# Second normalised rows moved from VectorE to ScalarE, and the projection of step 6 split straight from PSUM

## The reference

```
x = x + attention(layernorm(x), ctx)           # 16 heads of 64, 128 keys each
h = layernorm(x)                               # (x - mean) / sqrt(var + 1e-5)
logits = h @ Wg.T + bg                         # 16 experts, the best two are taken
x = x + sum over the two of weight_e * (gated(h @ Wgu[e] + bgu[e]) @ Wd[e] + bd[e])
```

## Time and profile before

| | us |
|---|---|
| median of 3 runs | 682.69 |
| lowest and highest | 680.43, 684.36 |
| the profiled execution | 684.96 |
| its span (first to last instruction) | 683.2 |

### The profile page before, as it was taken

One profiled execution on the slowest core, in us unless ns is written; L12 is line 12 of the kernel. 1 busy time (PEld: TensorE's weight loads), 2 busy tenths in 40 slices (PEclk: granted clock), 3 DMA queues, 4 the chain that ended last, 5 costly groups with the idle time before them and its releaser, 6 DMA issues.

```text
span 683.2 us, 20288 instructions
## 1 busy us (share of the span) xinstructions
PE 580.7 (85%) x6823; PEld 468.9 (69%) x6824; DVE 553.7 (81%) x1534; ACT 509.3 (75%) x1411; POOL 450.6 (66%) x551
## 2 busy tenths in 40 slices
PE   0787899999999999999999999998873898989900
PEld 0456688888888888888888888886762476666600
DVE  5776799899898998989989999887995387778605
ACT  0665698999999999999999999986971276767600
POOL 2353557678788787887878878874536157777740
PEclk9977899999999999999999999999996899999955
DMA  8700385007003300600700420181000243333139
GB/s 237 199 1 1 109 319 200 1 10 258 20 11 141 128 10 32 245 9 11 259 19 10 180 89 11 68 266 22 17 8 26 60 108 96 94 87 90 47 93 279
DMA packets 58962, 66.12 MB, mean 97 GB/s; under 512 B 6084, under 2 KB 38620, under 8 KB 58868
## 3 DMA queue, kind: packets, MB, share of 16 engines
q1 hardware_dynamic: 45268, 52.13, 23.7%
q0 software_dynamic: 4608, 8.47, 3.7%
q10 hardware_dynamic: 8992, 4.30, 2.3%
HBM read 19.09 MB, written 46.83 MB: 96 GB/s over the span
## 4 chain that ended last, share of the span: by engine, by line
PE 66%; DVE 14%; issue 8%; DMA 4%; ACT 2%; POOL 2%; SPq 1%; ACTq 1%; POOLq 0%; DVEq 0%
PE bank L1068 15%; PE bank L1069 14%; PE bank L1070 14%; PE bank L1157 9%; PE bank L1207 4%; PE bank L1232 3%; PE bank L1240 2%; DMA ctx_sb<-results 2%; DVE o_nat L949 2%; DMA ctx_sb<-in_ctx_dram 2%; PE bank L1289 2%; PE bank L1267 1%; DVE y L944 1%; DVE oT L883 1%; ACT v L424 1%
## 5 line engine op out<-in xcount | busy, mean ns | idle before, releaser
L476 ACT ACTIVATE probs<-bank,nbias 128x128 f32<-128x128 f32 x512 | 146.0, 368 | 4.1
L592 POOL TENSOR_TENSOR qk<-qkf,zeros 128x512 f16<-128x512 f32 x90 | 115.9, 1287 | 46.8 <-ACT qkf L419 45.4
L679 POOL DMA_INDIRECT results<-z,stage x80 | 80.9, 1011 | 43.4 <-ACT z L513 24.8
L595 POOL TENSOR_TENSOR qk<-qkf,qk 128x512 f16<-128x512 f32 x90 | 104.2, 1158 | 7.1
L908 DVE TENSOR_TENSOR pT<-bank,pT 128x512 f16<-128x512 f32 x128 | 87.7, 685 | 16.0 <-ACT pT L488 13.5
L1068 PE MATMUL bank<-qk 64*128 64x128 f16 x512 | 95.5, 222 | 0.0
L1070 PE MATMUL bank<-qk 64*128 64x128 f16 x512 | 94.4, 219 | 0.0
L1069 PE MATMUL bank<-qk 64*128 64x128 f16 x512 | 94.3, 219 | 0.0
L1157 PE MATMUL bank<-ident,probs 128*128 128x128 f32 x512 | 87.2, 295 | 1.9 <-DVE pT L908 1.9
L887 DVE TENSOR_REDUCE qmax<-bank 128x4 f32<-128x512 f32 x128 | 87.3, 682 | 1.2 <-PE bank L1070 1.1
L488 ACT ACTIVATE pT<-bank 128x512 f16<-128x512 f32 x128 | 76.9, 601 | 11.0 <-PE bank L1157 7.1
(11 more groups left out here) (202 smaller groups left out, 1890.4 us busy)
## 6 DMA issues: line engine op xcount, KB each, us to landing
places<-z SPq DMA_DIRECT2D x8, 4160.0 KB
stage<-places SPq DMA_DIRECT2D x80, 65.0 KB, 1.9
ctx_sb<-results SPq DMA_DIRECT2D x16, 256.0 KB, 5.4
ctx_sb<-in_ctx_dram ACTq DMA_DIRECT2D x4, 512.0 KB, 10.6
stage<-in_L_ffn_Wgu_dram SPq DMA_DIRECT2D x1, 2048.0 KB, 8.7
out_dram<-x_sb ACTq DMA_DIRECT2D x8, 256.0 KB, 5.3
stage<-in_L_xattn_W_qkv_dram SPq DMA_DIRECT2D x3, 512.0 KB, 6.6
results<-z,stage POOLq DMA_INDIRECT x80, 2.3
```

Of the source, the lines that this page charges most:

```text
L476: last = nc.scalar.activation(probs[:, b, k, :], score_bank[b][:, k * P:(k + 1) * P], ACT.Exp, bias=nbias[:, b, k:k + 1], scale=exp_scale)
L592: nc.gpsimd.tensor_tensor(qk_item(par, t, HI), each, zeros[:, :].rearrange("p (i n) -> p i n", i=2), ALU.add).then_inc(s["qk_high"], 1)
L595: nc.gpsimd.tensor_tensor(qk_item(par, t, LO), each, qk_item(par, t, HI), ALU.subtract).then_inc(s["qk_split"], 1)
L679: nc.gpsimd.indirect_dma_start(out=results, out_offset=bass.IndirectOffsetOnAxis(ap=to, axis=0), in_=z[:, (u - 5) % NZ, t, :], in_offset=None,
```

## The change

Piece 6 of each pair's queries and keys joins `DIRECT`. And the two row tiles of y are made by ACT, at the end of its step 7, as scale * x + bias with scale `rstd2` and bias `shift2` = -mean * rstd, for which POOL gets a new function `row_shift2` behind `inverse_root` in step 6. DVE no longer makes y; its casts L980 wait for ACT's `y_ok`.

```diff
-        DIRECT = (1, 4)
+        DIRECT = (1, 4, 6)
...
+                    if r == 7 and pair_live(p - 1):
+                        wait(act, "shift2_ok", p)
+                        wait(act, "yT_mm", p - 1)
+                        wait(act, "yhalf", p * 2 - 2)
+                        wait(act, "ylow", p * 2 - 2)
+                        for j in range(2):
+                            nc.scalar.activation(y[:, j, :], x_sb[:, p * 2 - 2 + j, :], ACT.Identity, bias=shift2[:, j:j + 1],
+                                                 scale=rstd2[:, j:j + 1]).then_inc(s["y_ok"], 1)
                     if ORDER[r] == "PREP" and pair_live(p + 2):
...
+            def row_shift2(q):
+
+                nc.gpsimd.tensor_tensor(under2[:, :], zeros[:, 0:2], mv2[:, :, 0], ALU.subtract).then_inc(s["under2_ok"], 1)
+                wait(pool, "rstd2_ok", q + 1)
+                wait(pool, "under2_ok", q + 1)
+                nc.gpsimd.tensor_tensor(shift2[:, :], under2[:, :], rstd2[:, :], ALU.mult).then_inc(s["shift2_ok"], 1)
...
                         inverse_root("stat2_agg", p * 2, mv2, var_eps2, rstd2, "rstd2_ok", adds)
+                        row_shift2(p - 1)
...
-                    if r == 7 and pair_live(p - 1):
-                        wait(dve, "rstd2_ok", p)
-                        wait(dve, "yT_mm", p - 1)
-                        wait(dve, "ylow", p * 2 - 2)
-                        for j in range(2):
-                            nc.vector.tensor_scalar(y[:, j, :], x_sb[:, p * 2 - 2 + j, :], mv2[:, j, 0:1], rstd2[:, j:j + 1],
-                                                    ALU.subtract, ALU.mult).then_inc(s["y_ok"], 1)
```

More of the change, by code:

```diff
@@ L129, in xattn_moe_kernel @@
         under = sb("under", [P, 2])
+        shift2 = sb("shift2", [P, 2])
+        under2 = sb("under2", [P, 2])
         zeros = sb("zeros", [P, 512])
@@ L183, in xattn_moe_kernel @@
         score_mm qmax_ok nbias_ok exp_ok pt_mm pt_hi pt_lo pv_mm rsum_ok o_ok ot_mm ot_hi ot_lo out_mm
-        x1_ok stat2 stat2_agg rstd2_ok y_ok yhalf ylow yT_mm lg_mm rank_mm
+        x1_ok stat2 stat2_agg rstd2_ok under2_ok shift2_ok y_ok yhalf ylow yT_mm lg_mm rank_mm
         best_ok best_at_ok choice_ok onehot_ok chosen_ok egap_ok
```

## The result

| | before | changed |
|---|---|---|
| median of 4 runs, us | 682.71 | 672.59 |
| lowest and highest | 680.43, 684.36 | 670.17, 674.92 |
| profiled execution, us | 684.96 | 670.17 |
| its span, us | 683.2 | 668.4 |

The two profiled executions differ by 14.8 us. That is more than the change, and the start explains it: the scores of pair 2 begin at 107.2 us before and at 103.2 after. Other executions begin pair 2 anywhere between 102.1 and 107.7 us over all versions (the kernel before, another time, 103.0; the changed kernel 102.9 to 107.2), by what some steps of pairs 0 and 1 took. So 4.0 us of the 14.8 are chance, and the comparison has to be made pair by pair.

A forecast was written before the change was run, and what follows sets the result against it. The prediction took PE as the bound; 12 steady pairs at 0.58 us (-7.0), pair 15 (-0.3) and the tail (+0.8) gave -6.5 us, so 676.2 us from a median of 682.69, range 673.0 to 681.0.

The forecast's parts named there:

- PE sets the pace, and step 0 has two holes of 0.29 and 0.45 us: Attention pairs: PE bounds them; step 0 loses 0.74 us waiting for DVE's y and oT, and could last 3.28.
- The casts, 0.58 of 0.74: DVE's casts of y: the second waits for POOL's L595, so 0.58 of 0.74 us per pair is gained.
- rival A: Casts of y on DVE are not held up: 0.74 us gained in 12 pairs, 674.3 us; chance 0.15.
- Pair 2 nothing, pair 15 0.3: Pairs outside the steady twelve: pair 2 gains nothing, pair 15 a net 0.3 us.
- The tail, 0.8 lost: Last y of the attention stage: two short POOL instructions and ACT's slower y cost 0.8 us.
- Piece 6 costs nothing, 0.6 us to spare: DVE's added L915 in step 6 ends 0.6 us before PE's projection in step 7 needs it: cost 0.
- POOL is off the chain there: POOL loses L592 and L595 of piece 6, 2.42 us per pair, which by itself gains nothing.
- ACT takes y at no cost: ACT's y, some 0.9 us, delays its oT, exponentials and copy pT; cost 0, upper end 0.9 us.
- The shift is there 0.35 us before it is asked for: POOL's `shift2` for y is ready at 304.3, 0.35 us before ACT asks for it.
- Rival S: ACT becomes the bound: a pair takes 28.6 us, 0.3 more; +4.4 in all, 687.1 us; chance 0.07.
- Rival N: Another wait replaces the hole in step 0; all but the last pair's loss given back: 682.5 to 683.5; chance 0.13.
- Rival C: Both casts of y wait for POOL's L595: 0.38 us gained in 12 pairs, 678.6 us; chance 0.15.

The follow-up runs named there:

- e4: The changed kernel with ACT making both row tiles of y twice; 718.42 us, ratio 0.9962 to the kernel before.
- e9: The changed kernel with DVE's casts of y waiting until POOL has made the high half of piece 7; 714.51 us, ratio 0.9899 to the kernel before.
- e5: The changed kernel, but for the last two pairs DVE makes y and the second shift is not issued; 668.71 us, ratio 0.9790 to the kernel before.
- e1: The kernel before with piece 6 direct, y still on DVE; 714.50 us, ratio 0.9887 to the kernel before; on the third chip 714.06, 0.9923.
- e2: The changed kernel with piece 6 back on POOL, y still made by ACT; 708.19 us, ratio 0.9803 to the kernel before.
- e3: The kernel before with piece 7 direct, y still on DVE; 704.51 us, ratio 0.9750 to the kernel before; on the third chip 704.50, 0.9775.

## Why the prediction was too high

*PE sets the pace, and step 0 has two holes of 0.29 and 0.45 us*: right. Both closed. There was a third that I did not look for: from the transposes of y to the next product with v it was 307.10 to 307.43 before (not among the rows shown) and 297.29 to 297.50 now, 0.12 us less. In the code that product waits for o_nat, which DVE ended at 307.28, 0.15 before it; so this hole too was y's lateness on DVE. Together the two intervals from the last projection matmul to L1218 went from 1.53 to 0.68 us, 0.85, which is the 0.83 of the step within reading. My floor of 3.28 was so 0.10 too high.

*The casts, 0.58 of 0.74*: this is the step that failed. I had the second cast lose to L595, with POOL's two instructions where they stood before. They do compete: in e4, where L616 starts 0.02 us behind the first cast, the first goes through and the second waits, 1.46 us for the two, as I had predicted it (305.61 to 307.1); in e9 it is 1.50. But in the changed kernel the shift's two short instructions stand ahead of POOL's L609. I had the casts 0.73 us and L595 0.83 us behind the start of the scores; measured are 0.72 for the casts and 0.96 for L612, with the second cast at 0.96 too. It went first, the two took 0.52 us, and L612 took 1.29 instead of 1.16. That 0.13 us decides is read from the times of these traces; no run took the shift's instructions away alone. So the outcome is that of rival A (674.3), though not by its reason, that the casts are not held up at all. The term is 0.83 x 12 = 10.0 us in place of 7.0: of the 0.25 us per pair 0.16 are the cast that did not lose and some 0.1 the third hole.

*Pair 2 nothing, pair 15 0.3*: measured 0.53 (3.71 to 3.18) and 0.61 (its seven steps 22.49 to 21.88). Another 0.8 us.

*The tail, 0.8 lost*: the piece that I worked out, from L559 to the end of y, is 1.36 to 2.14, 0.78 us. y came 1.15 later behind the last scores in the first two traces; the rest is when POOL got to L569 at all, 18.65 to 20.0 us behind the last scores over five traces, between scatters. The end of the execution lay 0.3 us later in the changed kernel in the first pair of traces, 1.0 later in the pair with e5. Mechanism right; the share that reaches the end is known only within these two.

The sum by these steps: 10.0 + 0.5 + 0.6 - 0.3 = 10.8 us, or 10.3 with the whole 0.8, against the medians' 10.1.

*Piece 6 costs nothing, 0.6 us to spare*: right, 0.60 in the first trace, but 0.12 on the second chip. *POOL is off the chain there*: wrong. In the kernel before POOL went without a pause from L592 of piece 6 at 300.60 to the end of L595 at 306.87, and step 0 follows that end; in e1 it waited 2.35 us for DVE ahead of L557. Once y has left DVE this no longer counts: e2 has step 0 at 3.18 without piece 6. *ACT takes y at no cost*: right. y started 0.49 us behind the start of the copy of v and waited for nothing; how much ACT has to spare no run shows. *The shift is there 0.35 us before it is asked for*: 294.73 against 295.01, 0.28.

Rival S (ACT the bound) did not come. Rival N is out: no other wait opened, and PE is busy without a gap. Rival C needed both casts to lose to L595; in no trace do both casts of a pair take long.

On the Trainium skill's rule ("SBUF — State Buffer", section "SBUF: two separate sides"): VectorE and GpSimd shut each other out for whole instructions here, as it says. 0.60 us for two y alone, 1.52, 1.67 and 2.29 beside POOL; 0.52 for two casts in the changed kernel, 1.46 and 1.50 when one of them comes behind L612. The rule was right, and I applied it with POOL's instruction 0.13 us too early. Its other side, "ScalarE: Activation LUTs", section "Rules for kernel authors", prefers VectorE for multiply and add: true of the instruction alone (0.60 against 0.88), and with POOL quiet the two kinds differ by 0.16 us per pair the other way, since DVE, not ACT, stands next to the bound.

What stays open. e1 gained 5.6 to 8.1 us by its two ratios, though its steady pairs are only 0.13 us shorter than those of the first trace of the kernel before. No trace of that kernel was taken on those two chips. On the second chip, where ACT and DVE go on late behind PE as they do on e1's, POOL's two instructions come later behind the scores and its pairs are 29.0 us; if they were so there too, the gain is accounted for, as the relief of POOL that the prediction put at nothing. And e3 took 3.1 us less than the changed kernel beside it on the third chip; the two intervals overlap. Its trace there is 4.6 us shorter: pair 2 begins 2.4 us earlier, the next twelve pairs give 1.9 back, pairs 14 and 15 are 0.8 shorter, and the part behind the last scores 3.2, of which 1.6 is y's earlier end. No run separated the edit's share from chance.

## What to carry to other kernels

Where two engines share a port, ask first which of them works beside the instruction that looks slow: moving the neighbour (one constant, e3) did as much as moving the instruction. When such a meeting is decided by who asks first, forecast it from the times at which both ask after the change, with every short instruction that the edit puts ahead of either, and keep both results in the range. In a pipeline that drains, the engine which is best in the steady part need not be so in the last round; e5 treats that one on its own.

## Of the hardware, not expected

A cast that asks while one of POOL's large instructions runs ends 0.15 us behind that instruction's end, whatever it waited: in 0.32 us here, 0.50 and 0.57 in the changed kernel on the third and second chip, 0.98 in e2, 1.30 in e9. Where the first cast had waited so for L609, the second always went ahead of L612 and took 0.28.

L855 of DVE (2048 wide, the low halves of expert weights, in step 0 of pair 1) took 3.28 us in the kernel before, where POOL's L595 of piece 7 had begun 0.03 us earlier and took 1.16, and 2.34 in both traces of e3, which has no such L595. POOL's L592 behind it took 2.78 and 2.13, and 1.27 alone. That step took 5.8 and 5.9 us in e3 and 6.4 to 7.0 in the kernels before and changed.

On the three slower chips ACT and DVE start late once or twice a pair, here in the kernel before on the second:

```profile
316.16 0.18 DVE L912 RECIPROCAL rsum<-bank 128x4 f32<-128x4 f32 x1 [0.94 <-PE bank L1070]
```

```profile
316.20 0.38 ACT L468 ACTIVATE oT<-bank 128x256 f16<-128x256 f32 x1 [0.58 <-PE bank L1207]
```

PE's L1207 had started at 315.19, 1.0 us earlier. Both engines wait for PE and go on within 0.04 us of each other, so what comes late is PE's signal and not ACT. Every trace with the longer expert stage has it in each pair from 4 to 13, the five others never. No run looked for the cause.
